# Two batches' own probabilities side by side: one 128x128 transpose in place of two in a fused Perceiver block

## The chip, the cores and the metric

The kernel runs on one core of one Trainium2 chip. The metric is device time of one execution in microseconds, lower is better. It is measured by repeated executions; one more execution was recorded by the profiler, and everything said of single instructions comes from that one.

## The reference, cut to what matters

The block has three parts in a row, each with a layer norm before it and a residual sum behind it: cross attention to a long context, causal self attention, and a mixture of eight experts of which two are used for each token. There are 8 batches of 64 tokens, width 256, 16 heads of 16.

```python
x = x + _L0_xattn_ref(_layernorm(x), ctx_1024, ctx_1024, ...)      # 1601 keys a batch
x = x + _L0_attn_ref(_layernorm(x), in_proj, out_proj)
x = x + _L0_ffn_ref(_layernorm(x), Wg, bg, W1, b1, W2, b2)         # 8 experts, top 2

# _L0_attn_ref, per batch and head, 64 x 64:
scores = jnp.einsum('bhqd,bhkd->bhqk', q / math.sqrt(D), k)
scores = jnp.where(causal[None, None], scores, -jnp.inf)
attn = jax.nn.softmax(scores, axis=-1)
out = jnp.einsum('bhqk,bhkd->bhqd', attn, v)
```

The change is in the self attention alone, between its softmax and its product with v.

## The kernel before, in words

**Tiles and steps.** Two batches make a tile of 128 token rows, so there are 4 tiles (0 to 3). The cross attention of a tile runs in 26 steps: for each of its two batches, 13 steps over blocks of up to 128 keys (k = 0 to 12; step s = 13 x batch + k). TensorE (PE) does in each step, in this order: the shift rows (L1382) and the scores (L1396) of the step, then "units" of other work, then `weigh` (L1216), the product of the last step's probabilities with the values. ScalarE (ACT) makes the exponentials (L739), GpSimd (POOL) adds them up in `prob_sum` (L490, four pieces a step). The exponential of a step waits for the sum of two steps before. In the last batch VectorE (DVE) does the sums. The denominators of a batch (`denominators`, L1415) are taken on PE in step k = 1 of the next batch, behind the last sum.

**Units.** A unit is a small piece of work that fills one PSUM bank and is read out by ACT or by DVE: "K" and "V" project keys and values of the batch to come, "M" finds score maxima (read by DVE at L923), "X" is the shift (L1256, behind DVE's `shift` at L865), "VL" are the last values. Between them stands the self attention and the router of the tile before, as a chain of units at steps written out by hand in `CHAIN_AT` (tiles 1 and 2), `CHAIN_AT_LAST` (tile 3) and `CHAIN_ALONE` (the tail behind tile 3, beside the first expert). So the chain of tile t runs within tile t + 1, and the program has it four times. The chain is: y1 (output projection), xt1, qk, v (projections), s0 and s1 (own scores of the two batches), the t units, o0 and o1 (product with v), y2, xt2, router, gt, b2.

**Banks.** Units take banks 2 to 6 in turn; a unit waits until the one that had its bank five units before has been read out. Tile 3 takes banks 4 to 6 in turn in its second half, the tail takes 6, 2, 7, 3. The first unit of a tile waits for all of the tile before.

**The softmax of the own scores.** DVE adds the mask to a batch's scores (L940), takes the row maxima (L841), subtracts them (L842); ACT takes the exponential in place (L670); two steps behind the scores DVE sums and divides the rows (L847 to L849) and raises `rows2_ready`. The result is `soft`, 128 rows by [2 batches, 8 head pairs, 64 keys]. A row is (one of two heads, query). The product with v needs keys on the rows, so the t units turn it.

**The t units.** Batch 0 is turned in t00 and t01 (step 12; step 11 in tile 3), batch 1 in t10 and t11 (step 14; step 13 in tile 3), all four at step 7 of the tail. A unit turns four 128x64 pieces into 64x128 and puts them on the upper (batch 0) or lower (batch 1) 64 rows of its bank. Batch 0's use the transpose operation (L1330, one pass of PE each). Batch 1's write rows 64 to 127 and are ordinary products with the identity (L1332), which for 32-bit data run as two passes each. ACT then copies 64 x 512 values a unit to `probs2` (L648), and o0 and o1 read that.

Of the kernel before, what the change touches and what calls it, by code (L numbers as in the profile page):

```python
# [12 lines left out]
P = 128  # L13
# [52 lines left out]
def in_order(counts):  # L66
    return {k: range(sum(n for j, n in counts.items() if j < k), sum(n for j, n in counts.items() if j <= k))
            for k in counts}
# [34 lines left out]
CHAIN_AT = {3: ["y1"], 5: ["xt1"], 6: ["qk", "v"], 8: ["s0"], 10: ["s1"], 12: ["t00", "t01"], 14: ["t10", "t11"],  # L103
            15: ["o0"], 16: ["o1"], 18: ["y2"], 20: ["xt2"], 21: ["router"], 24: ["gt"], 25: ["b2"]}

CHAIN_AT_LAST = {2: ["y1"], 4: ["xt1"], 5: ["qk", "v"], 7: ["s0"], 9: ["s1"], 11: ["t00", "t01"],
                 13: ["t10", "t11"], 15: ["o0", "o1"], 17: ["y2"], 19: ["xt2"], 20: ["router"], 23: ["gt"],
                 24: ["b2"]}
CHAIN_ALONE = {1: ["y1"], 2: ["xt1"], 3: ["qk"], 5: ["s0", "s1", "v"], 7: ["t00", "t01", "t10", "t11"],
               8: ["o0", "o1"], 9: ["y2"], 11: ["xt2"], 12: ["router"], 15: ["gt"], 16: ["b2"]}  # L110
ALONE_BANKS = [6, 2, 7, 3]
DONE_TILES = TT - 1
# [16 lines left out]
READ_BY_ACT = {"p1", "p2", "p3", "v", "V", "VL", "X", "xt1", "qk", "t00", "t01", "t10", "t11", "xt2", "router", "gt"}  # L129


class Units:
# [3 lines left out]
    def __init__(self, before, batch_after, chain, own=True, after_shift=len(V_AT[SHIFT_AT]), banks=RING_BANKS,  # L136
# [8 lines left out]
        for s in range(STEPS):  # L145
# [3 lines left out]
            for kind, u in row:  # L149
# [5 lines left out]
                     for n in range(len(order))]  # L155

# [125 lines left out]
def perceiver_kernel(nc, x, ctx_t, w_t, wg_t, biases, bo_row, bg_row, w1, b1, w2, b2, eye, masks, causal, out):  # L282
    stack = ExitStack()
    with stack:
# [48 lines left out]
        soft = sb("soft", [P, 2, G * PAIRS, Q])  # L333
# [265 lines left out]
        def _(act):  # L599
# [14 lines left out]
            def unit(units, n, kind, u, t, b, parity):  # L614
# [30 lines left out]
                elif kind[0] == "t":  # L645
                    bi, g = int(kind[1]), int(kind[2])
                    rows = slice(bi * Q, bi * Q + Q)
                    nc.scalar.activation(probs2[rows, g * 512:g * 512 + 512], src[rows, :], ACT.Copy)\  # L648
                        .then_inc(read_act, 1)
# [14 lines left out]
            def own_exponentials(units, s, t):  # L664

                for kind in units.chain.get(s - 1, []):
                    if kind in ("s0", "s1"):
                        bi = int(kind[1])
                        act.wait_ge(soft_ready, 2 * t + bi + 1)
                        nc.scalar.activation(soft[:, bi], soft[:, bi], ACT.Exp).then_inc(soft_exp_done, 1)  # L670
# [137 lines left out]
        def _(dve):  # L808
# [31 lines left out]
            def subtract_maxima(bi):  # L840
                link(nc.vector.tensor_reduce(neg_max2[:, bi], soft[:, bi], AX.X, ALU.max, negate=True))  # L841
                nc.vector.tensor_tensor(soft[:, bi], soft[:, bi], by_row(neg_max2[:, bi]), ALU.add).then_inc(soft_ready, 1)  # L842

            def divide_rows(bi, count):

                dve.wait_ge(soft_exp_done, count)
                link(nc.vector.tensor_reduce(row_sums2[:, bi], soft[:, bi], AX.X, ALU.add))  # L847
                link(nc.vector.reciprocal(row_sums2[:, bi], row_sums2[:, bi]))
                nc.vector.tensor_tensor(soft[:, bi], soft[:, bi], by_row(row_sums2[:, bi]), ALU.mult).then_inc(rows2_ready, 1)  # L849
# [765 lines left out]
```

## Time and profile before

| | us |
|---|---|
| median of 3 runs | 663.91 |
| lowest and highest | 663.18, 666.14 |
| the profiled execution | 663.55 |
| its span, first to last instruction | 661.7 |

Busy shares of the span: TensorE 95%, VectorE 72%, ScalarE 50%, GpSimd 46%. The span falls into a start (to 41 us), tile 0 (to 140), tile 1 (to 250), tile 2 (to 360), tile 3 (to 451), a tail with the fourth chain and the first expert (to about 494), and the seven other experts. PE is named apart as PE (products) and PEld (loading of the stationary operand, which overlaps). The distance between the starts of two products is what one costs when they stand in a row; the duration of a record is longer, as products are pipelined.

### The profile page before, as it was taken

The page shows a single profiled execution, that of the slowest core. Times are in us where ns is not written, and L with a number is a line of the kernel's source. Part 1 is how long each engine was busy: PE and PEld are TensorE (multiplying, and loading weights), DVE is VectorE, ACT ScalarE, POOL GpSimd, SP SyncE. Part 2 cuts the span into 40 slices and gives each one's busy share as a digit, 9 for nine tenths or more (in the row PEclk, how much of TensorE's full clock was granted, in tenths as well). Part 3 has the DMA queues.
Part 4 walks back from the last instruction along what each step waited for, and adds up shares of the span by engine and source line. Part 5 has one row for each costly group of instructions (what it writes and reads, how often), then busy time and mean ns, then how long its engine had stood idle before and what let it go on. Part 6 is the DMA issues. An engine that isn't in the chain of part 4 may idle for free.

```text
span 661.7 us, 15583 instructions
## 1 busy us (share of the span) xinstructions
PE 630.8 (95%) x6304; PEld 532.8 (81%) x6312; DVE 475.3 (72%) x878; ACT 329.4 (50%) x541; POOL 301.9 (46%) x386
## 2 busy tenths in 40 slices
PE   7989999999989989989998999978989999999997
PEld 4778878868877868877887888757879999999997
DVE  4887757667687678688777868686777666656753
ACT  4355655555554555446555545463654444444421
POOL 2138788897686688678678768200000000000000
PEclk9999999999989999999999999998989999999999
DMA  6311110100010010011110000423003302330000
GB/s 184 134 50 52 28 51 26 51 27 26 27 52 1 27 50 27 26 27 51 27 27 26 2 1 2 152 106 127 1 1 128 128 26 104 127 127 0 0 0 33
DMA packets 13285, 34.11 MB, mean 52 GB/s; under 512 B 1563, under 2 KB 10532, under 8 KB 11044
## 3 DMA queue, kind: packets, MB, share of 16 engines
q1 hardware_dynamic: 13188, 33.19, 15.1%
q8 instruction: 46, 0.75, 0.5%
q14 instruction: 19, 0.16, 0.1%
q0 software_dynamic: 32, 0.01, 0.0%
HBM read 32.67 MB, written 0.52 MB: 50 GB/s over the span
## 4 chain that ended last, share of the span: by engine, by line
PE 74%; DVE 13%; issue 5%; ACT 3%; POOL 3%; DMA 2%; SPq 0%; POOLq 0%; DVEq 0%; ACTq 0%
PE bank L1207 46%; PE bank L1396 8%; PE bank L1216 7%; PE bank L1382 4%; PE bank L1277 3%; POOL prob_sum L490 3%; DVE maxes L923 3%; DVE ctx_lo L474 2%; DMA raw<-in_w 1%; ACT k_hi L626 1%; DVE k_lo L904 1%; PE bank L1332 1%; PE bank L1320 1%; PE bank L1304 1%; DVE prob_sum L490 1%
## 5 line engine op out<-in xcount | busy, mean ns | idle before, releaser
L490 POOL TENSOR_TENSOR prob_sum<-probs,prob_sum 128x256 f32<-128x256 f32 x336 | 270.6, 837 | 71.4 <-ACT probs L739 66.4
L739 ACT ACTIVATE probs<-bank 128x1024 f32<-128x1024 f32 (+1 forms) x104 | 106.6, 1025 | 111.6 <-PE bank L1396 99.2
L923 DVE TENSOR_REDUCE maxes<-bank 128x1 f32<-128x400 f32 (+1 forms) x256 | 129.5, 564 | 20.3 <-PE bank L1277 19.8
L721 ACT ACTIVATE h_raw<-bank,b_sb 128x512 f32<-128x512 f32 (+2 forms) x72 | 46.2, 642 | 106.5 <-PE bank L1207 106.3
L904 DVE SCALAR_TENSOR_TENSOR k_lo<-bank,bias_sb,k_hi 128x400 fp32r<-128x400 f32 (+2 forms) x64 | 40.5, 632 | 48.6 <-ACT k_hi L626 48.6
L1207 PE MATMUL bank<-w_hi,h_hi 128*128 128x256 f32 x256 | 73.6, 288 | 0.8 <-DVE h_lo L1142 0.8
L1207 PE MATMUL bank<-w_lo,h_hi 128*128 128x256 f32 x256 | 72.9, 285 | 0.0
L1207 PE MATMUL bank<-w_hi,h_lo 128*128 128x256 f32 x256 | 72.8, 284 | 0.0
L1216 PE MATMUL bank<-probs,v_sb 128*32 128x128 f32 (+1 forms) x1664 | 68.1, 282 | 1.0 <-ACT probs L739 0.5
L1141 DVE CAST h_hi<-h_raw 128x512 fp32r<-128x512 f32 (+2 forms) x72 | 28.5, 396 | 55.5 <-ACT h_raw L721 54.1
L1207 PE MATMUL bank<-wv_hi,ctx_hi 128*128 128x256 f32 (+1 forms) x208 | 65.3, 314 | 2.6 <-DVE maxes L923 2.4
L1396 PE MATMUL bank<-qbd_hi,k_hi 64*128 64x256 f32 (+1 forms) x416 | 67.1, 318 | 0.0
L1277 PE MATMUL bank<-k_hi,qbd_hi 64*128 64x400 f32 (+1 forms) x256 | 58.5, 444 | 1.0 <-DVE qbd_hi L881 0.4
L1396 PE MATMUL bank<-qbd_lo,k_hi 64*128 64x256 f32 (+1 forms) x416 | 59.0, 279 | 0.0
L1396 PE MATMUL bank<-qbd_hi,k_lo 64*128 64x256 f32 (+1 forms) x416 | 58.9, 278 | 0.0
L1207 PE MATMUL bank<-wv_lo,ctx_hi 128*128 128x256 f32 (+1 forms) x208 | 58.7, 282 | 0.0
L1207 PE MATMUL bank<-wv_hi,ctx_lo 128*128 128x256 f32 (+1 forms) x208 | 58.4, 281 | 0.0
L629 ACT ACTIVATE v_sb<-bank 128x256 f32<-128x256 f32 (+1 forms) x104 | 39.7, 382 | 37.1 <-PE bank L1207 33.4
L626 ACT ACTIVATE k_hi<-bank,bias_sb 128x400 fp32r<-128x400 f32 (+2 forms) x64 | 38.1, 596 | 38.7 <-PE bank L1207 38.7
L1207 PE MATMUL bank<-xn_hi,w_hi 128*128 128x512 f32 (+2 forms) x144 | 55.0, 382 | 0.0
L1207 PE MATMUL bank<-xn_hi,w_lo 128*128 128x512 f32 (+2 forms) x144 | 54.8, 380 | 0.0
L1207 PE MATMUL bank<-xn_lo,w_hi 128*128 128x512 f32 (+2 forms) x144 | 54.6, 379 | 0.0
(155 smaller groups left out, 1389.8 us busy)
## 6 DMA issues: line engine op xcount, KB each, us to landing
raw<-in_w SPq DMA_DIRECT2D x16, 1024.0 KB, 6.8
ctx_raw<-in_ctx_t SPq DMA_DIRECT2D x16, 400.0 KB, 3.6
ctx_raw<-in_ctx_t SPq DMA_DIRECT2D x8, 402.0 KB, 3.8
ctx_raw<-in_ctx_t SPq DMA_DIRECT2D x8, 399.0 KB, 3.6
w_sb<-in_w_t SPq DMA_DIRECT2D x1, 1280.0 KB
w_raw<-in_w_t SPq DMA_DIRECT2D x2, 256.0 KB, 4.7
result<-x_all SPq DMA_DIRECT2D x4, 128.0 KB, 2.0
x_all<-in_x SPq DMA_DIRECT2D x1, 384.0 KB, 4.1
```

Of the source, the lines that this page charges most:

```text
L490: ins = engine.tensor_tensor(prob_sum[0:ROWS[k], cols], probs[0:ROWS[k], s % 2, cols], acc[0:ROWS[k]], ALU.add)
L626: nc.scalar.activation(k_hi[parity][:, g, EDGE[c]:EDGE[c + 1]], src[:, EDGE[c] - CH[c]:CW], ACT.Identity, bias=bias_sb[:, 1, g:g + 1]).the ...
L629: nc.scalar.activation(v_sb[0:ROWS[u], u * D:u * D + D], src[0:ROWS[u], 0:D], ACT.Copy).then_inc(read_act, 1)
L721: nc.scalar.activation(h_raw[:, c % 2, 0:width], bank[:, at, 0:width], ACT.Gelu, bias=b1_sb[:, bass.ds(e, 1), c:c + 1].rearrange("p a b -> ...
L739: nc.scalar.activation(probs[0:ROWS[k], s % 2, :].rearrange("p (g n) -> p g n", g=G), bank[0:ROWS[k], score_bank(b, k):score_bank(b, k) + ...
L904: nc.vector.scalar_tensor_tensor(out=k_lo[parity][:, g, EDGE[c]:EDGE[c + 1]], in0=src[:, EDGE[c] - CH[c]:CW], scalar=bias_sb[:, 1, g:g + 1 ...
L923: nc.vector.tensor_reduce(maxes[:, g * PAIRS + j, c:c + 1], src[:, 0:width], AX.X, ALU.max).then_inc(read_dve, 1)
L1141: link(nc.vector.tensor_copy(h_hi[:, c % 4, 0:width], h_raw[:, c % 2, 0:width]))
L1207: last = nc.tensor.matmul(dst, lhs, rhs, start=(start and n == 1), stop=(stop and n == 3 * len(pairs)), **more)
L1216: ins = nc.tensor.matmul(dst_bank[32 * j:32 * j + 32, (at + g) * P:(at + g + 1) * P], lhs(g, j), p_rows[:, m * P:(m + 1) * P], start=(star ...
L1277: ins = nc.tensor.matmul(dst[:, 0:width], qbd_hi[rows, parity, g, 2 * i:2 * i + 2, :].rearrange("p s q -> p (s q)"), k_hi[parity][rows, g, ...
L1396: ins = nc.tensor.matmul(bank[0:rows, score_bank(b, k) + r, g * RH * Q:(g + 1) * RH * Q], stays, moves, start=False, stop=(part == 2), ski ...
```

## The change

`soft` becomes [8 head pairs, 2 batches, 64 keys], so that the two batches' rows for a head pair lie side by side as 128 columns. One transpose of 128x128 turns both: the upper 64 rows of the result are batch 0's keys, the lower 64 batch 1's. The units t00, t01, t10, t11 become t0 and t1, which stand where t10 and t11 stood; at the steps of t00 and t01 nothing stands. Both wait for both batches' rows. The copies by ACT take 128 rows. DVE's and ACT's instructions on `soft` keep their number and size, but now step over the other batch's 64 columns. A tile has two units fewer, so the turn of the banks shifts; in the tail the banks of gt and b2 are set by a table.

```diff
-CHAIN_AT = {..., 10: ["s1"], 12: ["t00", "t01"], 14: ["t10", "t11"],
+CHAIN_AT = {..., 10: ["s1"], 14: ["t0", "t1"],
-CHAIN_AT_LAST = {..., 9: ["s1"], 11: ["t00", "t01"],
-                 13: ["t10", "t11"], 15: ["o0", "o1"], ...
+CHAIN_AT_LAST = {..., 9: ["s1"], 13: ["t0", "t1"],
+                 15: ["o0", "o1"], ...
-CHAIN_ALONE = {..., 5: ["s0", "s1", "v"], 7: ["t00", "t01", "t10", "t11"],
+CHAIN_ALONE = {..., 5: ["s0", "s1", "v"], 7: ["t0", "t1"],
+GATE_BANKS = {"gt": 3, "b2": 6}
...
+        if banks is ALONE_BANKS:
+            for n, kind in enumerate(order):
+                self.bank[n] = GATE_BANKS.get(kind, self.bank[n])
...
-        soft = sb("soft", [P, 2, G * PAIRS, Q])
+        soft = sb("soft", [P, G * PAIRS, 2, Q])
...
                 elif kind[0] == "t":
-                    bi, g = int(kind[1]), int(kind[2])
-                    rows = slice(bi * Q, bi * Q + Q)
-                    nc.scalar.activation(probs2[rows, g * 512:g * 512 + 512], src[rows, :], ACT.Copy)\
-                        .then_inc(read_act, 1)
+                    g = int(kind[1])
+                    nc.scalar.activation(probs2[:, g * 512:g * 512 + 512], src, ACT.Copy).then_inc(read_act, 1)
...
-                        nc.scalar.activation(soft[:, bi], soft[:, bi], ACT.Exp).then_inc(soft_exp_done, 1)
+                        nc.scalar.activation(soft[:, :, bi, :], soft[:, :, bi, :], ACT.Exp).then_inc(soft_exp_done, 1)
...
-                link(nc.vector.tensor_reduce(row_sums2[:, bi], soft[:, bi], AX.X, ALU.add))
+                link(nc.vector.tensor_reduce(row_sums2[:, bi], soft[:, :, bi, :], AX.X, ALU.add))
...
                 elif kind[0] == "t":
-                    bi, g = int(kind[1]), int(kind[2])
-                    pe.wait_ge(rows2_ready, 2 * t + bi + 1)
+                    g = int(kind[1])
+                    pe.wait_ge(rows2_ready, 2 * t + 2)
                     for j in range(PAIRS):
-                        turned, own_rows = dst[bi * Q:bi * Q + Q, j * P:j * P + P], soft[:, bi, g * PAIRS + j, :]
-                        if bi == 0:
-                            ins = nc.tensor.transpose(turned, own_rows, ident[:, :])
-                        else:
-                            ins = nc.tensor.matmul(turned, own_rows, ident[:, :], start=True, stop=True)
+                        ins = nc.tensor.transpose(dst[:, j * P:j * P + P],
+                                                  soft[:, g * PAIRS + j].rearrange("p b q -> p (b q)"), ident[:, :])
...
-                    units.wait_read_act(pe, read_act, f"t{bi}1")
+                    units.wait_read_act(pe, read_act, "t1")
```

Of DVE's instructions (L841, L842, L847, L849, L940) one stands for all; the others change in the same way.

On TensorE, step 12 of tile 1 stood so before: the scores of a short block of 65 keys, t00 and t01 (`ident,soft`), and the value unit.

```order
L1396 MATMUL bank<-qbd_hi,k_hi 65x256 x2
L1396 MATMUL bank<-qbd_lo,k_hi 65x256 x2
L1396 MATMUL bank<-qbd_hi,k_lo 65x256 x2
L1330 MATMUL bank<-ident,soft 64x128 x8
L1207 MATMUL bank<-wv_hi,ctx_hi 128x256
L1207 MATMUL bank<-wv_lo,ctx_hi 128x256
```

And so now, with line numbers of the changed file:

```order
L1394 MATMUL bank<-qbd_hi,k_hi 65x256 x2
L1394 MATMUL bank<-qbd_lo,k_hi 65x256 x2
L1394 MATMUL bank<-qbd_hi,k_lo 65x256 x2
L1208 MATMUL bank<-wv_hi,ctx_hi 128x256
L1208 MATMUL bank<-wv_lo,ctx_hi 128x256
```

The eight transposes are gone, and the value unit stands right behind the scores. On TensorE in step 14 of tile 1, t10 and t11 stood between the key unit (`ctx`, `wk`) and the unit of the last values:

```order
L1207 MATMUL bank<-ctx_hi,wk_hi 128x402
L1207 MATMUL bank<-ctx_lo,wk_hi 128x402
L1207 MATMUL bank<-ctx_hi,wk_lo 128x402
L1332 MATMUL bank<-ident,soft 64x128 x8
L1207 MATMUL bank<-wv_hi,ctx_hi 65x256
L1207 MATMUL bank<-wv_lo,ctx_hi 65x256
```

Now t0 and t1 stand in the same place:

```order
L1208 MATMUL bank<-ctx_hi,wk_hi 128x402
L1208 MATMUL bank<-ctx_lo,wk_hi 128x402
L1208 MATMUL bank<-ctx_hi,wk_lo 128x402
L1329 MATMUL bank<-ident,soft 128x128 x8
L1208 MATMUL bank<-wv_hi,ctx_hi 65x256
L1208 MATMUL bank<-wv_lo,ctx_hi 65x256
```

Nothing has moved there but the form: 128 rows of result in place of 64, by the transpose operation.

## Rows read from the trace of the kernel before

**Rows 1.** The page, part 1: busy us, share of span, instructions
```profile
PE 630.8 (95%) x6304; PEld 532.8 (81%) x6312; DVE 475.3 (72%) x878; ACT 329.4 (50%) x541; POOL 301.9 (46%) x386
```
**Rows 2.** Busy us of each engine in tiles 1 and 2 and most of 3
```profile
146.50:410.00 263.50, 254.50 (x3001) 212.98 (x3005) 204.10 (x352) 139.32 (x224) 198.61 (x251) 0.99 0.09 25
```
**Rows 3.** Chain that ended last, tile 1: start us, us, what
```profile
192.83 0.99 PE bank L1330 x8
...
202.24 1.96 PE bank L1332 x16
```
**Rows 4.** The two t lines: duration ns min/median/max, first and last start us
```profile
L1330 PE MATMUL bank<-ident,soft x32: 271/273/300, 192.8 to 473.5; 128*64 128x128 f32 x32
L1332 PE MATMUL bank<-ident,soft x64: 272/273/323, 202.2 to 476.0; 128*64 128x128 f32 x64
```
**Rows 5.** Timeline of PE, tile 1: start us, us [idle before <-releaser]
```profile
161.56 0.38 PE L1231 MATMUL bank<-ident,xn 128*128 128x128 f32 x2
...
192.76 1.06 PE L1330 MATMUL bank<-ident,soft 128*64 128x128 f32 x8
193.58 0.36 PE L1207 MATMUL bank<-wv_hi,ctx_hi 128*128 128x256 f32 x1
...
202.24 1.96 PE L1332 MATMUL bank<-ident,soft 128*64 128x128 f32 x16
204.13 0.34 PE L1207 MATMUL bank<-wv_hi,ctx_hi 128*65 128x256 f32 x1
```
**Rows 6.** Timeline of PE, tile 2, step 12
```profile
303.03 1.04 PE L1330 MATMUL bank<-ident,soft 128*64 128x128 f32 x8 [0.22 <-DVE soft L849]
303.82 0.36 PE L1207 MATMUL bank<-wv_hi,ctx_hi 128*128 128x256 f32 x1
```
**Rows 7.** Timeline, tile 1, steps 12 to 15, POOL, PE, DVE
```profile
194.35 4.25 POOL L490 TENSOR_TENSOR prob_sum<-probs,prob_sum 65x256 f32<-65x256 f32 x4 [0.17 <-ACT probs L739]
...
199.86 0.65 PE L1216 MATMUL bank<-prob_sum,ones_f 128*32 128x128 f32 x16
...
201.61 2.02 DVE L923 TENSOR_REDUCE maxes<-bank 128x1 f32<-128x402 f32 x4
...
206.18 2.03 DVE L923 TENSOR_REDUCE maxes<-bank 128x1 f32<-128x402 f32 x4 [0.76 <-PE bank L1277]
```
**Rows 8.** Timeline, tile 3, steps 10 to 14, POOL, DVE, PE
```profile
406.77 10.37 POOL L490 TENSOR_TENSOR prob_sum<-probs,prob_sum 128x256 f32<-128x256 f32 x12 [0.21 <-ACT probs L739]
...
408.18 1.54 DVE L865 TENSOR_TENSOR shift<-ident,neg_max 128x1024 bf16<-128x1024 f32 x1
...
410.67 0.38 PE L1256 MATMUL bank<-shift,ones_bf 128*128 128x512 bf16 x1 [0.16 <-issue]
...
418.92 0.65 PE L1216 MATMUL bank<-prob_sum,ones_f 128*32 128x128 f32 x16
```
**Rows 9.** Timeline of the tail, step 7, DVE and PE
```profile
473.47 0.69 DVE L849 TENSOR_TENSOR soft<-soft,row_sums 128x512 f32<-128x512 f32 x1
...
474.30 1.93 PE L1332 MATMUL bank<-ident,soft 128*64 128x128 f32 x16 [0.52 <-DVE soft L849]
```
**Rows 10.** Two ACT copies out of PSUM, columns as in group 4
```profile
L648 ACT ACTIVATE probs<-bank x16: 577/592/597, 194.2 to 476.3; 64x512 f32<-64x512 f32 x16
L633 ACT ACTIVATE shift_rows<-bank x16: 576/597/626, 38.7 to 411.4; 128x512 bf16<-128x512 f32 x16
```
**Rows 11.** Two DVE lines, columns as in group 4
```profile
L904 DVE SCALAR_TENSOR_TENSOR k_lo<-bank,bias_sb,k_hi x64: 618/634/639, 11.1 to 394.6; 128x400 fp32r<-128x400 f32 x32, 128x402 fp32r<-128x402 f32 x16, 128x399 fp32r<-128x399 f32 x16
L855 DVE SCALAR_TENSOR_TENSOR masked<-bank,mask_sb,masked x8: 483/484/485, 96.0 to 452.3; 128x256 f32<-128x256 f32 x8
```
**Rows 12.** Two stretches: PE, PEld, DVE, ACT, POOL busy, clock, DMA share, GB/s
```profile
185.80:189.10 3.30, 3.30 (x30) 2.57 (x30) 3.23 (x4) 0.39 (x1) 3.11 (x4) 0.50 0.46 124
192.80:196.20 3.40, 3.40 (x47) 2.91 (x46) 3.40 (x4) 2.71 (x7) 3.23 (x4) 1.00 0.02 5
```
**Rows 13.** Timeline of PE ahead of the first of these stretches
```profile
183.95 2.00 PE L1320 MATMUL bank<-k_t,qbd 128*128 128x64 f32 x16 [1.77 <-issue]
```

More of the change, by code:

```diff
@@ L101 @@
 LAST_V_AT = 1
-CHAIN_AT = {3: ["y1"], 5: ["xt1"], 6: ["qk", "v"], 8: ["s0"], 10: ["s1"], 12: ["t00", "t01"], 14: ["t10", "t11"],
+CHAIN_AT = {3: ["y1"], 5: ["xt1"], 6: ["qk", "v"], 8: ["s0"], 10: ["s1"], 14: ["t0", "t1"],
             15: ["o0"], 16: ["o1"], 18: ["y2"], 20: ["xt2"], 21: ["router"], 24: ["gt"], 25: ["b2"]}
[L106 to L109, printed above, removed]
+CHAIN_AT_LAST = {2: ["y1"], 4: ["xt1"], 5: ["qk", "v"], 7: ["s0"], 9: ["s1"], 13: ["t0", "t1"],
+                 15: ["o0", "o1"], 17: ["y2"], 19: ["xt2"], 20: ["router"], 23: ["gt"], 24: ["b2"]}
+CHAIN_ALONE = {1: ["y1"], 2: ["xt1"], 3: ["qk"], 5: ["s0", "s1", "v"], 7: ["t0", "t1"],
                8: ["o0", "o1"], 9: ["y2"], 11: ["xt2"], 12: ["router"], 15: ["gt"], 16: ["b2"]}
 ALONE_BANKS = [6, 2, 7, 3]
+GATE_BANKS = {"gt": 3, "b2": 6}
 DONE_TILES = TT - 1
@@ L126, in both_tiles @@
     return [("M", ROW_TILES * u + r) for u in pairs for r in range(ROW_TILES)]
-READ_BY_ACT = {"p1", "p2", "p3", "v", "V", "VL", "X", "xt1", "qk", "t00", "t01", "t10", "t11", "xt2", "router", "gt"}
+READ_BY_ACT = {"p1", "p2", "p3", "v", "V", "VL", "X", "xt1", "qk", "t0", "t1", "xt2", "router", "gt"}
 class Units:
@@ L840, in subtract_maxima @@
             def subtract_maxima(bi):
-                link(nc.vector.tensor_reduce(neg_max2[:, bi], soft[:, bi], AX.X, ALU.max, negate=True))
-                nc.vector.tensor_tensor(soft[:, bi], soft[:, bi], by_row(neg_max2[:, bi]), ALU.add).then_inc(soft_ready, 1)
+                link(nc.vector.tensor_reduce(neg_max2[:, bi], soft[:, :, bi, :], AX.X, ALU.max, negate=True))
+                nc.vector.tensor_tensor(soft[:, :, bi, :], soft[:, :, bi, :], by_row(neg_max2[:, bi]), ALU.add).then_inc(soft_ready, 1)
             def divide_rows(bi, count):
                 dve.wait_ge(soft_exp_done, count)
-                link(nc.vector.tensor_reduce(row_sums2[:, bi], soft[:, bi], AX.X, ALU.add))
+                link(nc.vector.tensor_reduce(row_sums2[:, bi], soft[:, :, bi, :], AX.X, ALU.add))
                 link(nc.vector.reciprocal(row_sums2[:, bi], row_sums2[:, bi]))
-                nc.vector.tensor_tensor(soft[:, bi], soft[:, bi], by_row(row_sums2[:, bi]), ALU.mult).then_inc(rows2_ready, 1)
+                nc.vector.tensor_tensor(soft[:, :, bi, :], soft[:, :, bi, :], by_row(row_sums2[:, bi]), ALU.mult).then_inc(rows2_ready, 1)
             def own_heads(src, read, count):
@@ L938, in unit @@
                 elif kind in ("s0", "s1"):
-                    nc.vector.tensor_tensor(soft[:, int(kind[1])], src.rearrange("p (n k) -> p n k", k=Q),
+                    nc.vector.tensor_tensor(soft[:, :, int(kind[1]), :], src.rearrange("p (n k) -> p n k", k=Q),
                                             causal_sb[:, :].unsqueeze(1).broadcast_to([P, G * PAIRS, Q]),
```

## The prediction

> **What bounds the kernel now.** I read the page's busy shares first: PE is busy 95% of the span, DVE 72%, ACT 50%, POOL 46% [rows 1]. The shares of the stretch in which three of the four chains run say more: from 146.5 to 410 us PE is busy 254.5 of 263.5 us, DVE 204.1, POOL 198.6 and ACT 139.3 [rows 2]. So PE is the bound there, but two others are at about three quarters, and each can be the one waited for at single steps. Next I asked whether the instructions that the change touches are on the path. The chain that ended last runs through both of tile 1's groups, 0.99 us at L1330 and 1.96 us at L1332 [rows 3]. The reader is to see that no wait stands between them and their neighbours in tile 1: behind L1330 the value unit starts at once, at 193.58 [rows 5]. Work taken out of such a row is time taken out, until something else is late.
>
> **The price of one transpose.** A record lasts 273 ns at both lines [rows 4], but they overlap. L1330's eight span 1.06 us, so their distance is (1.06 - 0.27) / 7 = 0.11 us; L1332's sixteen give (1.96 - 0.27) / 15 = 0.11 us [rows 5]. One pass is thus 0.11 us, and batch 1's products take two passes each. The new form is 128x128. The trace has it at L1231, where two in a row span 0.38 us with the same 273 ns each, again 0.11 us apart [rows 5, 4]. Bounds for the new one: 0.109, as L1231 has it, and 0.27, if eight in a row did not overlap at all. I take 0.11, since L1231 is the same operation with the same operand sizes; two in a row are thin evidence for eight, but L1332's sixteen keep the same distance. A tile has 8 + 16 = 24 passes before and 8 after: 16 x 0.11 = 1.76 us less of PE a tile, 7.0 us for four chains. That is the ceiling; now what each place lets through.
>
> The Trainium skill, page "TensorE: Matmul & The Clock Gate", section "Part 4: PE-mode transpose", gives about 275 ns for a transpose of 128x128 in one kernel's context. The trace agrees as to the duration and not as to the distance. Were that figure the cost of each, a tile would save 16 x 0.275 = 4.4 us and the kernel would end some 11 us below my forecast.
>
> **Tiles 1 and 2.** Step 12 loses t00 and t01: from 192.76 to 193.58, 0.82 us [rows 5]. In tile 2 the same unit starts at 303.03 after 0.22 us of waiting for DVE's division of batch 0, and the next one at 303.82 [rows 6]. The wait goes too: 0.79 + 0.22 = 1.01 us. Step 14 keeps eight passes of sixteen, 8 x 0.11 = 0.87 us less in each. Sum 0.82 + 1.01 + 2 x 0.87 = 3.57 us.
>
> What is late next? First POOL. Its sum of step 12 ends at 194.35 + 4.25 = 198.60, and PE takes the denominators at 199.86 [rows 7]. Their place moves up by 0.82 to 199.04, so 0.44 us of the slack remains. Then DVE. In step 14 it reduces the four maxima in 2.02 us from 201.61; that is behind the denominators and moves with them [rows 7]. In step 15 its next maxima start at 206.18 after 0.76 us idle. That start may move by 0.87 more than DVE's earlier work does; 0.76 of it is idle time, so at most 0.11 us is lost there, and DVE idles again soon after. I count nothing for it. The new wait, on both batches' rows instead of one's, stands where batch 1's stood already, so nothing is queued behind a later event than before. I went through the bank of each unit: from step 14 on each follows the same kind as before, and the five that follow the two removed units get banks that have been free for longer.
>
> **Tile 3.** Step 11 loses 0.8 us, but PE then comes to X, which waits for DVE's shift: that ends at 408.18 + 1.54 = 409.72, and X started at 410.67, with about 0.25 us between release and start [rows 8]. X can move to about 409.98, so 0.69 us come through. Step 13 gives 0.87. POOL adds up steps 10, 11 and 12 in one run of 10.37 us, to 417.14, and the denominators stand at 418.92 [rows 8]: 1.56 us earlier is 417.36, just behind the sum. Sum 1.56 us, with 0.2 us of cover left; the range must allow for its failing.
>
> **Tail.** Here batch 0's eight passes ran while DVE was still dividing batch 1's rows (473.47 to 474.16), and batch 1's started at 474.30 after a wait of 0.52 us for that [rows 9]. Taking batch 0's away only lengthens the wait. Batch 1's sixteen become eight behind the same event: 0.87 us, not 1.76.
>
> **ACT and DVE.** ACT makes two copies of 128 rows for four of 64. Rows cost it nothing: 64x512 takes 592 ns and 128x512 takes 597 [rows 10]. It gets 1.2 us a tile back, which PE and POOL hide, as nobody waits for it in steps 12 and 14; if that cover were gone it would be a further gain. DVE's and ACT's instructions on `soft` now step over 64 columns after every 64. Is that dearer? L855 reads a PSUM bank in just such pieces: 484 ns for 256 columns. L904 reads without gaps: 634 ns for 400. Both have the same kind of scalar operand. The difference, 150 ns for 144 columns, is 1.04 ns a column, which leaves 484 - 266 = 218 ns and 634 - 416 = 218 ns of fixed cost [rows 11]. So gaps cost nothing that can be seen. Nothing that reads and writes SBUF in such pieces stands in the trace, so zero is taken by the nearest row, and the other end is a rival below.
>
> **The sum.** 3.57 + 1.56 + 0.87 = 6.0 us. The profiled execution took 663.55, so it would take 657.55. The median of the runs is 0.36 us above it: **657.9 us**, 0.9% less.
>
> **Rivals.**
> 1. *The gain in step 12 does not come through.* If POOL or DVE is late at the places above, because DVE's operations and POOL's stretch when they fall together in a new way, the 0.82, 1.01 and 0.69 us are lost and 3 x 0.87 + 0.87 = 3.5 us remain: 660.4 us. For it speaks the thin cover, 0.44 and 0.2 us. Against it: POOL began both of those runs after waiting for an exponential, 0.17 and 0.21 us [rows 7, 8], so it was not behind when they started, and in tile 1 it has idle time again behind 198.60, until the denominators are taken.
> 2. *The gaps in `soft` cost DVE and ACT time, and the kernel is slower.* There are 10 DVE operations of 512 columns and 2 of ACT a tile. In the tail nearly all of them follow one another ahead of t0, and in tile 2 PE waits for them at step 12 [rows 6, 9]; I reckon 30 on the path in all. The change loses from 6.0 / 30 = 0.2 us an operation on. If a gap halved the rate, each would take 0.53 us more: 30 x 0.53 = 16 us, less 6.0, gives about 674 us. Rows 11 speak against it.
> 3. *More half-speed stretches.* The granted clock was 0.50 from 185.8 to 189.1 us, behind 1.77 us of idle PE [rows 12, 13], and there are more such stretches later in the run. Each can cost up to half of its 3.4 us, 1.7 us. Two more would give 657.9 + 3.4 = 661.3; one fewer 656.2. In the stretch behind tile 1's eight transposes the clock stayed at 1.00 [rows 12], so the transposes do not bring one on here. The same section of the Trainium skill says that the full clock does not engage for transposes; by that the eight new ones, in place of sixteen plain products, would invite one more such stretch a tile, and the trace does not bear it out.
> 4. *Passes are dearer in the new form.* At 0.27 us each the eight take 2.2 us, 1.3 more than I take, four times: 663 us, no change.
> 5. *All of the ceiling comes through*, with a little from ACT: 663.9 - 7.2 = 656.7 us; with one half-speed stretch fewer 655.0.
>
> **How the numbers follow.** Forecast, with its own spread from 656.0 to 659.8 (rival 5 without the clock lies in it): 0.60. Rival 1: 0.13. Rival 2, at any size that undoes the gain or worse: 0.06. Rival 3 upward: 0.08, downward 0.05. Rival 4: 0.03. A gain larger than the ceiling for a reason that I don't see: 0.05. The range takes in rivals 1, 3 and 5: **655.0 to 662.0**. Faster or slower by 0.5%, 3.3 us, is about what a measurement of this kernel can tell from no change; the lines are at 660.6 and 667.2. Below the first lie the forecast, rival 3 downward, the larger gain and half of rival 1: 0.76. Within: half of rival 1, most of 3 upward, 4, and the mild half of 2: 0.19. Above: 0.05.
>
> **What would show it.** In the profile after, eight records a tile at the t line (L1329), 32 in all, 0.11 us apart, eight in 1.04 us; rival 4 would show as 2.2 us. ACT's copies: 8 of about 597 ns. DVE's lines on `soft`: means as before, 0.68 to 0.69 us where POOL is quiet; rival 2 would show there at once. The value unit of step 12 right behind the scores, and the denominators of tile 3 not waiting for POOL; rival 1 shows as an idle PE ahead of them with POOL as the releaser. The distance between the same step of tile 1 and tile 2 shorter by about 1.7 us. What would make me wrong: a wait in a place that I did not look at, above all between steps 15 and 25, where I take all work to move up as one.

## The result and the profile after

The changed kernel takes 658.37 us (median of 4 runs, 656.94 to 659.16) against 663.92 before: a ratio of 0.9929, 95% interval 0.9900 to 0.9959. Two later measurements of the same kernel, each with more executions of the kernel before beside it, gave 658.67 against 662.81 (ratio 0.9936, 0.9913 to 0.9960) and 658.14 against 662.75 (0.9938, 0.9911 to 0.9965). Some executions take 6 to 13 us longer at a lower granted clock, whatever the kernel, and one of an experiment below took 2016 us; medians, means and ratios here are without them. So the change is faster by 0.6 to 0.7% by the ratios and by 4.1 to 5.5 us by the medians, where the forecast was 6.0 us. The time was forecast at 657.9, and the range 655.0 to 662.0 holds all three.

The page of the changed kernel's profiled execution: its span, part 1 (busy us, share of the span, instructions) and the engines' shares of part 4, the chain that ended last:

```profile
span 655.1 us, 15447 instructions
PE 626.0 (96%) x6248; PEld 526.5 (80%) x6248; DVE 474.7 (72%) x878; ACT 324.2 (49%) x533; POOL 301.2 (46%) x386
PE 73%; DVE 13%; issue 6%; POOL 3%; ACT 3%; DMA 2%; POOLq 0%; DVEq 0%; SPq 0%; ACTq 0%
```

Against [rows 1] PE has lost 4.8 us of busy time and ACT 5.2; DVE's 878 instructions take as long as before. The new t line and ACT's copies of its result in the changed kernel (duration ns min/median/max, first and last start us) answer to [rows 4, 10]:

```profile
L1329 PE MATMUL bank<-ident,soft x32: 272/273/331, 201.3 to 470.9; 128*128 128x128 f32 x32
L650 ACT ACTIVATE probs<-bank x8: 591/597/603, 202.0 to 471.2; 128x512 f32<-128x512 f32 x8
```

The timeline of PE in tile 1 of the changed kernel (start us, us) answers to [rows 5]; the first two lines are step 12, the last two step 14:

```profile
192.30 0.28 PE L1394 MATMUL bank<-qbd_hi,k_lo 64*65 64x256 f32 x2
192.51 0.38 PE L1208 MATMUL bank<-wv_hi,ctx_hi 128*128 128x256 f32 x1
...
201.28 1.14 PE L1329 MATMUL bank<-ident,soft 128*128 128x128 f32 x8
202.24 0.33 PE L1208 MATMUL bank<-wv_hi,ctx_hi 128*65 128x256 f32 x1
```

The value unit of step 12 stands right behind the scores. In step 14 the t units hold PE for 202.24 - 201.28 = 0.96 us, where it was 204.13 - 202.24 = 1.89 [rows 5].

Where the time went is read best from the starts of the exponentials, as each ends one step of PE. Here are those of steps 12 to 15 of tile 1, from ACT's timeline (start us, us, and at the end the idle time ahead and what ended it), before (L739) and after (L740):

```profile
193.25 1.03 ACT L739 ACTIVATE probs<-bank 65x1024 f32<-65x1024 f32 x1
196.18 1.03 ACT L739 ACTIVATE probs<-bank 128x1024 f32<-128x1024 f32 x1 [0.69 <-PE bank L1396]
199.97 1.02 ACT L739 ACTIVATE probs<-bank 128x1024 f32<-128x1024 f32 x1 [1.40 <-PE bank L1396]
206.89 1.02 ACT L739 ACTIVATE probs<-bank 128x1024 f32<-128x1024 f32 x1 [1.41 <-PE bank L1396]
```
```profile
192.98 1.02 ACT L740 ACTIVATE probs<-bank 65x1024 f32<-65x1024 f32 x1
195.21 1.03 ACT L740 ACTIVATE probs<-bank 128x1024 f32<-128x1024 f32 x1 [0.93 <-PE bank L1394]
199.01 1.02 ACT L740 ACTIVATE probs<-bank 128x1024 f32<-128x1024 f32 x1 [1.41 <-PE bank L1394]
205.00 1.02 ACT L740 ACTIVATE probs<-bank 128x1024 f32<-128x1024 f32 x1 [1.42 <-PE bank L1394]
```

The lead is 0.97 us at steps 13 and 14 and 1.89 at step 15, so step 14 gave 0.92. The lead was 0.26 to 0.27 at step 12, so the t units' leaving it gave 0.71. Done in the same way everywhere, for the first profile and for the one of the run `again` (for the tail, the starts of the first layer's activations ahead of it and behind it, in `again` alone, where both kernels have the same number of half-speed stretches between them):

| place | forecast us | first profile | second profile |
|---|---|---|---|
| tile 1, step 12 | 0.82 | 0.71 | 0.71 |
| tile 1, step 14 | 0.87 | 0.92 | 0.91 |
| tile 2, step 12 | 1.01 | 0.94 | 0.94 |
| tile 2, step 14 | 0.87 | 0.91 | 0.93 |
| tile 3, step 11 | 0.69 | 0.58 | 0.58 |
| tile 3, step 13 | 0.87 | 1.07 | 1.07 |
| tail | 0.87 | | 0.94 |
| sum | 6.00 | | 6.08 |

What else differs is the clock. Both profiles have a half-speed stretch in tile 2 that the profile before lacks; it costs 1.51 and 1.57 us of the 6. Two stretches of the changed kernel, one in tile 1 and this one in tile 2 (from and to us, length, busy us of PE, PEld, DVE, ACT and POOL, the granted clock, DMA share, GB/s):

```profile
185.80:189.10 3.30, 3.30 (x34) 2.57 (x34) 3.23 (x4) 0.38 (x1) 2.85 (x3) 0.50 0.45 124
295.10:298.40 3.30, 3.30 (x30) 2.66 (x29) 3.23 (x4) 0.38 (x1) 3.30 (x4) 0.50 0.45 124
```

At 0.50 the engine runs at 1.2 GHz, the lower of its two levels. The stretch in tile 1 is in both kernels [rows 12]. At the end of tile 3 the changed kernel has a longer one, some 10 us in one piece, in all three of its profiles; the profile before has two of 3.4 us there with full clock between them. The changed kernel, and the middle of that place in the kernel before, columns as above:

```profile
441.90:452.00 10.10, 8.65 (x71) 6.75 (x68) 7.30 (x14) 4.27 (x7) 0.00 (x0) 0.50 0.53 207
```
```profile
448.70:451.90 3.20, 1.47 (x33) 1.00 (x34) 1.93 (x3) 1.95 (x3) 0.00 (x0) 1.00 0.26 41
```

In the first profile a stretch in the tail, which the kernel before has at 486.1 us, is missing in turn; so its span is 6.6 us shorter, 655.1 for 661.7, where the medians differ by 5.5.

The timed executions say the same as these profiles. The mean granted clock of an execution is 0.987 over 18 of the changed kernel and 0.990 over the 55 of the kernel before that ran beside it and beside the experiments; 19 of the 55 reach 0.991 or more, and none of the 18 does. That is some 3 us more at half speed in each execution, worth 1.1 to 1.5 us by my estimate (0.45 us for each 0.001 of clock among the 55, and 1.5 us for a stretch of 3.4 us). It accounts for most of the way from the 6.1 us of the table to the 4.1 and 4.6 us of the two larger comparisons.

### The profile page after: what moved, and what is told of

Its sections match the earlier page's. It is cut to its first block, busy times and chain, and to the rows that moved or that the text cites. A ratio compares the mean times of both kernels' runs of the same rounds, so it can differ in the third digit from the quotient of the medians.

```text
span 655.1 us, 15447 instructions
## 1 busy us (share of the span) xinstructions
PE 626.0 (96%) x6248; PEld 526.5 (80%) x6248; DVE 474.7 (72%) x878; ACT 324.2 (49%) x533; POOL 301.2 (46%) x386
## 4 chain that ended last, share of the span: by engine, by line
PE 73%; DVE 13%; issue 6%; POOL 3%; ACT 3%; DMA 2%; POOLq 0%; DVEq 0%; SPq 0%; ACTq 0%
PE bank L1208 45%; PE bank L1394 8%; PE bank L1217 7%; PE bank L1380 4%; DVE maxes L924 3%; PE bank L1278 3%; POOL prob_sum L493 3%; DVE ctx_lo L477 1%; DMA raw<-in_w 1%; PE bank L1321 1%; DVE prob_sum L493 1%; ACT k_hi L629 1%; DVE k_lo L905 1%; DVE shift L866 1%; PE bank L1305 1%
## 5 line engine op out<-in xcount | busy, mean ns | idle before, releaser
L740 ACT ACTIVATE probs<-bank 128x1024 f32<-128x1024 f32 (+1 forms) x104 | 106.6, 1025 | 111.8 <-PE bank L1394 99.4
```

What stands on the lines that cost most here:

```text
L740: nc.scalar.activation(probs[0:ROWS[k], s % 2, :].rearrange("p (g n) -> p g n", g=G), bank[0:ROWS[k], score_bank(b, k):score_bank(b, k) + ...
```

## Experiments: is it the passes, and which of them?

**The layout alone.** The kernel before, with the new shape of `soft` and nothing else:

```diff
-        soft = sb("soft", [P, 2, G * PAIRS, Q])
+        soft = sb("soft", [P, G * PAIRS, 2, Q])
...
-                        turned, own_rows = dst[bi * Q:bi * Q + Q, j * P:j * P + P], soft[:, bi, g * PAIRS + j, :]
+                        turned, own_rows = dst[bi * Q:bi * Q + Q, j * P:j * P + P], soft[:, g * PAIRS + j, bi, :]
```

> The kernel before with the new layout of soft alone: [8 head pairs, 2 batches, 64 keys], all four t units at their old steps, with their old operations. Theory (gaps cost nothing): as before, 663.9 us within 1 us, and the means of the ten DVE operations and two ACT operations a tile as before (about 0.68 us where GpSimd is quiet, 0.63 us on ACT). Rival (gaps cost time): at 0.2 us an operation with some 30 on the path, 670 us; the means of those lines show it directly.

Measured: 661.71 us, against 662.81 for the kernel before beside it, ratio 0.9989 (0.9965 to 1.0012). DVE's and ACT's instructions on `soft` in that kernel, by tile (duration ns min/median/max):

```profile
L940 DVE TENSOR_TENSOR soft<-bank,causal_sb x8: 673/680/692, 178.4 to 467.8; 128x512 f32<-128x512 f32 x8
L842 DVE TENSOR_TENSOR soft<-soft,neg_max x8: 691/952/1206, 179.8 to 469.2; 128x512 f32<-128x512 f32 x8
L670 ACT ACTIVATE soft<-soft x8: 622/626/632, 181.2 to 469.9; 128x512 f32<-128x512 f32 x8
L849 DVE TENSOR_TENSOR soft<-soft,row_sums x8: 691/959/1239, 190.6 to 472.3; 128x512 f32<-128x512 f32 x8
```

And the same instructions in the kernel before, without gaps:

```profile
L940 DVE TENSOR_TENSOR soft<-bank,causal_sb x8: 675/680/692, 178.1 to 468.9; 128x512 f32<-128x512 f32 x8
L842 DVE TENSOR_TENSOR soft<-soft,neg_max x8: 692/959/1216, 179.5 to 470.3; 128x512 f32<-128x512 f32 x8
L670 ACT ACTIVATE soft<-soft x8: 622/626/632, 180.9 to 471.1; 128x512 f32<-128x512 f32 x8
L849 DVE TENSOR_TENSOR soft<-soft,row_sums x8: 691/955/1222, 190.3 to 473.5; 128x512 f32<-128x512 f32 x8
```

Line by line the medians are within 1% of each other; those of the maxima (L841) are 686 ns in both. Steps over 64 columns cost nothing here, on either engine; rival 2 is gone.

**The operation.** The changed kernel with the plain product for the transpose, of the same size and in the same place:

```diff
-                        ins = nc.tensor.transpose(dst[:, j * P:j * P + P],
-                                                  soft[:, g * PAIRS + j].rearrange("p b q -> p (b q)"), ident[:, :])
+                        ins = nc.tensor.matmul(dst[:, j * P:j * P + P],
+                                               soft[:, g * PAIRS + j].rearrange("p b q -> p (b q)"), ident[:, :],
+                                               start=True, stop=True)
```

> The changed kernel with the transpose operation replaced by the plain product with the identity, of the same 128x128: two passes for one. Theory (passes count, 0.11 us each): 8 x 0.11 = 0.87 us more in each of four chains, 658.4 + 3.5 = 661.9 us. Rival (what gave the gain is the lower number of instructions or of units, not passes): 658.4. Rival on the clock (transposes bring half-speed stretches on, products do not): fewer such stretches than with transposes.

**Each transpose twice.**

```diff
+                        for _ in range(2):
                             ins = nc.tensor.transpose(...)
```

> The changed kernel with each of the eight transposes issued twice to the same place. Theory: 8 x 0.11 = 0.87 us more a chain, 661.9 us, as the run with products; step 14 to 15 longer by 0.87 us in each tile. Rival (repeats are hidden by another engine): 658.4. Rival on the clock: more half-speed stretches than in the run with products, as there are 16 transposes a tile.

Measured: 661.27 us with products (ratio 0.9997, 0.9959 to 1.0034) and 660.60 with doubled transposes (0.9982, 0.9955 to 1.0008), against 658.67 for the changed kernel beside them (`again`). PE's timeline in step 14 of tile 1 (start us, us), first the kernel with products, then the one with doubled transposes:

```profile
201.66 2.05 PE L1329 MATMUL bank<-ident,soft 128*128 128x128 f32 x16
```
```profile
200.04 1.97 PE L1330 MATMUL bank<-ident,soft 128*128 128x128 f32 x16
201.77 0.36 PE L1208 MATMUL bank<-wv_hi,ctx_hi 128*65 128x256 f32 x1
```

Both have sixteen passes a tile. By the starts of the exponentials both keep the gain of step 12 (0.70 and 0.73 us in tile 1, 0.94 and 0.95 in tile 2) and lose that of step 14 (0.07 and 0.16 in place of 0.92). So the gain of step 14 is the number of passes: the doubled transposes need 201.77 - 200.04 = 1.73 us for sixteen, 0.11 us each in a row of sixteen. In tiles 1 and 2 the loss is 0.85 and 0.76 us each, near the 0.87; in tile 3 it is 0.98 and 0.88, and the tail gains 0.1 and 0.2 us over the kernel before where the changed kernel gains 0.94. That is some 3.5 and 3.2 us for the four chains, as expected.

The median times, 2.6 and 1.9 us above the changed kernel, fall short of that. In the mean the kernel with products is 3.7 us above (661.95 of 10 executions, 658.28 of all 18 of the changed kernel), the one with doubled transposes 2.1; but of the latter's ten executions four had a granted clock of 0.994, which none of the 18 reached. So the half-speed stretches, which differ between executions, hide part of the loss. The times alone would not have settled the question.

**Batch 0's units left out, in the tiles and in the tail.** In the kernel before:

```diff
-CHAIN_AT = {..., 10: ["s1"], 12: ["t00", "t01"], 14: ["t10", "t11"],
+CHAIN_AT = {..., 10: ["s1"], 14: ["t10", "t11"],
```

> The kernel before without t00 and t01 in the chains of tiles 1 to 3 (the turning of batch 0 is left out there, and o0 reads batch 1's rows instead); the tail as before. Theory: 0.82 + 1.01 + 0.69 = 2.5 us less, 661.4 us. Rival (that place is covered by GpSimd or VectorE): no change, 663.9.

```diff
-CHAIN_ALONE = {..., 7: ["t00", "t01", "t10", "t11"],
+CHAIN_ALONE = {..., 7: ["t10", "t11"],
```

> The kernel before without t00 and t01 in the tail alone (left out there: the turning of batch 0; o0 reads what the chain before left). Theory: they run while VectorE still divides batch 1's rows, so nothing is saved: 663.9 us, and the wait ahead of t10 grows from 0.5 to about 1.6 us. Rival: 0.87 us less, 663.0; by the timed runs alone these two can't be told apart, by the profile's timeline they can.

(This kernel also has the changed kernel's table of banks for gt and b2 in the tail, and o0 waits there for t11's copy.)

Without them in the tiles: 662.38 us, against 662.42 beside it, ratio 1.0006 (0.9959 to 1.0053). By the time it is no change. By the starts of the exponentials it is 0.72, 0.95 and 0.60 us less, 2.3 in all, just the share of step 12 in the changed kernel; a stretch of half speed that is 6.8 us long in tile 2 takes 3 us back in the profiled execution. The time was inconclusive, the profile was not. Without them in the tail: 663.17 us, ratio 1.0011 (0.9988 to 1.0035), and PE's timeline there shows the wait that the theory named (start us, us, in brackets the idle time ahead and its releaser):

```profile
473.06 1.93 PE L1336 MATMUL bank<-ident,soft 128*64 128x128 f32 x16 [1.60 <-DVE soft L853]
```

It was 0.52 us with them in place [rows 9]. Eight passes ahead of that event are free there. PE's timeline of the changed kernel has the same wait, and half of the work behind it:

```profile
470.08 1.06 PE L1329 MATMUL bank<-ident,soft 128*128 128x128 f32 x8 [1.61 <-DVE soft L850]
```

**How much further would it go?** The changed kernel with one of four transposes:

```diff
-                    for j in range(PAIRS):
+                    for j in range(1):
```

> The changed kernel with one of four transposes in each t unit; the turning of the other three head pairs is left out. Theory: 6 x 0.11 = 0.66 us less in each chain, 658.4 - 2.6 = 655.8 us. Rival: the cover that GpSimd had in tile 3 (0.2 us by the sum) is used up, and step 14 there waits for the sum of step 12: then 0.5 us of that does not come through, and the releaser of the denominators there is GpSimd.

Measured: 657.21 us in the median of four, ratio 0.9899 (0.9852 to 0.9947). Of 6 x 0.11 = 0.66 us a chain, 2.6 us in all, the median is 1.2 below the 658.4 of all 18 executions of the changed kernel; by the profile it is some 0.5, of which 0.35 lie in the tail. In step 14 the gain over the kernel before is 0.93 us in tiles 1 and 2, the same as with eight passes. The reason is in that kernel's timeline of PE, tile 1:

```profile
201.40 0.33 PE L1329 MATMUL bank<-ident,soft 128*128 128x128 f32 x1
201.88 0.33 PE L1329 MATMUL bank<-ident,soft 128*128 128x128 f32 x1 [0.15 <-DVE maxes L924]
202.36 0.33 PE L1208 MATMUL bank<-wv_hi,ctx_hi 128*65 128x256 f32 x1 [0.15 <-DVE maxes L924]
```

t0, t1 and the value unit need banks that DVE frees one by one, and they start 201.88 - 201.40 = 202.36 - 201.88 = 0.48 us apart whatever they hold. Four transposes take 0.44 us. So the changed kernel sits just at that floor, and fewer passes bring nothing in step 14. And in tile 3, where the gain was 1.19 us for 1.07, the same kernel's PE waits for the sum of POOL, as the rival had it:

```profile
415.04 0.64 PE L1217 MATMUL bank<-prob_sum,ones_f 128*32 128x128 f32 x16 [0.49 <-POOL prob_sum L493]
```

## Experiments: the idle time ahead of s1

The kernel before idles 1.77 us on PE ahead of s1 in tile 1 [rows 13], and a half-speed stretch stands behind it. PE's timeline of the changed kernel shows the same in tile 2, ahead of the stretch at 295.1:

```profile
293.56 2.30 PE L1321 MATMUL bank<-k_t,qbd 128*128 128x64 f32 x16 [1.77 <-issue]
```

Since t0 and t1 are not due before step 14, s1 can stand a step later:

```diff
-CHAIN_AT = {3: ["y1"], 5: ["xt1"], 6: ["qk", "v"], 8: ["s0"], 10: ["s1"], 14: ["t0", "t1"],
+CHAIN_AT = {3: ["y1"], 5: ["xt1"], 6: ["qk", "v"], 8: ["s0"], 11: ["s1"], 14: ["t0", "t1"],
```

> The changed kernel with the scores of the second batch (s1) one step later, at 11 in place of 10, in tiles 1 and 2; this has room because t0 waits at step 14 for both batches. In both profiles PE idles 1.77 us ahead of s1 for VectorE's spreading of the queries, and a half-speed stretch follows in tile 1. Theory: both idle times go, 658.4 - 3.5 = 654.9 us, and with one or two half-speed stretches fewer (1.5 us each) 652 to 653.5. Rival: VectorE is what is late there, and the wait comes back ahead of X or of t0: 658.

Measured: 654.47 us, ratio 0.9868 (0.9828 to 0.9909). That is near the 654.9 that I had for the idle times alone, and above the 652 to 653.5 with the stretches gone too. The wait ahead of s1 is gone, and so is the stretch: here PE's timeline of tile 1 (start us, us), and then busy times and clock of the stretch around it, with the columns as above. The granted clock is 1.00, which is 2.4 GHz:

```profile
184.86 0.28 PE L1394 MATMUL bank<-qbd_hi,k_lo 64*128 64x256 f32 x2
185.07 2.00 PE L1321 MATMUL bank<-k_t,qbd 128*128 128x64 f32 x16
```
```profile
184.00:190.00 6.00, 5.84 (x73) 4.78 (x69) 5.86 (x9) 3.14 (x5) 5.75 (x5) 1.00 0.23 68
```

Then four kernels side by side on one chip: the kernel before with the same move, the changed kernel with it once more, that with one more edit in the tail, and the changed kernel as it is.

> The kernel before (sixteen transposes and products in four units) with s1 one step later in tiles 1 and 2. Theory: the idle time ahead of s1 goes here too, and with it the half-speed stretches in tiles 1 and 2; against the changed kernel with the same move (654.5 us) it is slower by what the change gives by itself where no half-speed stretch differs: 1.6 + 1.9 + 1.6 + 0.9 = 6.0 us, so 660.5 us. Rival (the change gives less once the idle time is gone, or the move needs the change): the two are within 3 us.

> The changed kernel with s1 at step 11, once more beside the others. Theory: 654.5 us, and again no half-speed stretch in tiles 1 and 2. Rival (the absence of such stretches in its first profile was luck): one is there, and the time is 1.5 us more for each.

> As that, and in the tail PE does the first layer's chunk 6 of the first expert ahead of t0 instead of behind t1. PE idles 1.6 us there for VectorE's division; the chunk takes 1.05 us. Theory: 1.0 us less, 653.5 us. Rival: the chain of the tail is held later by something that does not move (xn, 0.8 us idle), and nothing is gained.

> The changed kernel beside these. 658.4 us; a half-speed stretch in tile 1 or 2 behind the idle time ahead of s1.

| kernel | median us | ratio to before (95%) |
|---|---|---|
| before, s1 at 11 | 658.72 | 0.9931 (0.9905 to 0.9957) |
| changed, s1 at 11 | 654.50 | 0.9870 (0.9777 to 0.9964) |
| the same, tail swapped | 655.20 | 0.9842 (0.9767 to 0.9917) |
| changed | 658.14 | 0.9938 (0.9911 to 0.9965) |

**The move alone.** It works without the change as well, by 0.7%, as much as the change itself. In none of the profiles of the three kernels with s1 at step 11, four in all, is there a half-speed stretch in tiles 1 and 2. Of the ten profiles with s1 at step 10, before and changed and the experiments above, eight have at least one. So the stretches of tiles 1 and 2 go with the idle time ahead of s1, whichever form the t units have. It is not certain to bring one on, since two of the ten profiles have none; and that it is the cause, and not something else that the move shifts, is not shown. The timed executions agree less clearly: the mean clock of the kernel before rises from 0.990 to 0.992 with the move, yet four of its nine executions are still at 0.989, so those still have more of the half speed somewhere.

The exponential of step 15 in tile 1 shows how the gain divides. In `before_s1` it starts 2.63 us earlier than in the kernel before (the start of the profile taken off). A half-speed stretch there is worth 1.5 us (the changed kernel's first profile and its third, which has none, part by that much at step 11), so 1.1 us of the 1.77 of idle time are gained for good. In the changed kernel less is gained: against its third profile, without a stretch, `s1_again` leads by 3.53 - 3.18 = 0.35 us only, and by 0.38 us more in tile 2, where I had expected 1.77 us in each. What PE waits for instead in that kernel, in steps 12 and 13 of tile 1:

```profile
195.36 0.39 PE L1380 MATMUL bank<-shift_rows,ones_bf 64*128 64x512 bf16 x2 [0.64 <-ACT probs L740]
...
197.42 0.64 PE L1217 MATMUL bank<-prob_sum,ones_f 128*32 128x128 f32 x16 [0.37 <-POOL prob_sum L493]
```

So of the 3.6 us by which the move betters the changed kernel 0.7 are the wait that it takes away, and most of the rest goes with the clock: both profiles of the changed kernel with the move have one stretch of 3.4 us at the end of tile 3 too, where the changed kernel has 10 us.

**The change on top of the move** gives 658.72 - 654.50 = 4.2 us, where I expected 6.0. By the medians that is no less than without the move (4.1 to 5.5 us), but it is made up in another way: without the move 6.1 us came off the steps and the clock took some back; here 4.5 us came off the steps. What fell away is step 12: with s1 a step later the removal there brings nothing, since the wait of 0.64 us for the exponential, above, has taken its place. The kernel before with the move has the eight passes there and no such wait, only the one for POOL (its timeline of PE, same place):

```profile
195.80 0.39 PE L1382 MATMUL bank<-shift_rows,ones_bf 64*128 64x512 bf16 x2
...
197.76 0.64 PE L1216 MATMUL bank<-prob_sum,ones_f 128*32 128x128 f32 x16 [0.38 <-POOL prob_sum L490]
```

What is left, by the exponentials, is step 14 (0.90 and 0.92 us), tile 3 (1.65) and the tail (1.06), 4.5 us.

**The tail swapped.** The edit puts one chunk of the first layer ahead of t0, to fill the 1.6 us of waiting:

```diff
             for s in range(LAST_ROWS_AT):
-                alone(s)
+                if s != 7:
+                    alone(s)
                 for c in FIRST_HIDDEN.get(s, []):
...
                     hidden(0, c, c % 2, 0, DONE_TILES)
+                if s == 7:
+                    alone(s)
```

It gave nothing that can be seen: the median is 655.20 against 654.50, the ratio is better, 0.9842 against 0.9870, and with four executions each (one of `s1_again` took 661.73 us) neither difference is clear of noise. Its timeline of PE around t0 and t1:

```profile
466.00 1.06 PE L1329 MATMUL bank<-ident,soft 128*128 128x128 f32 x8 [0.54 <-DVE soft L850]
467.89 0.17 PE L1337 MATMUL bank<-ident_bf,ones_bf 128*128 128x8 bf16 x1 [0.83 <-ACT probs L650]
```

The wait ahead of t0 shrank by 1.06 us, as meant. But the chunk had covered ACT's two copies between t1 and o0, and now PE waits 0.83 us for those. One more half-speed stretch at 468.7 us, which its profile has, cost 1.5 us there. No kernel of the study is shown to be faster than the changed one with s1 at step 11.

## The remaining expectation

> The changed kernel once more, for a second profile. 658 us. The starts of the exponentials, step by step, should move against the kernel before by 0.7 and 0.9 us in tile 1, 0.9 and 0.9 in tile 2, 0.6 and 0.9 in tile 3, as in its first profile; what differs between the two profiles should be only the half-speed stretches. Rival: the new half-speed stretch in tile 2 (295 us) belongs to the change; then it is there again.

The shares of the steps agree within 0.02 us between the two profiles. The stretch at 295 us was there again; but in the third profile of the changed kernel (`after_third`) neither it nor the one in tile 1 is there, and the kernel with the layout alone, which has the transposes of before, has one at 296.7 us. So it comes and goes with the execution. That the changed kernel has more of such stretches on average is shown above; what in the change brings them is open. The kernels with products, with doubled transposes and without batch 0's units in the tiles, which all leave step 12 without t units, have a mean clock of 0.986, 0.988 and 0.986; the kernels with the layout alone and with the tail alone changed have 0.991 and 0.989.

## Why the prediction was right, point by point

- **The bound.** PE was the one to shorten: outside the tail nearly every pass taken away came off the steps. Of the ceiling of 7.0 us 6.1 came through there, and the free half in the tail is the 0.87 that did not. In the timed runs 4.1 to 5.5 us are left, for the clock took some back.
- **Luck in the number.** The 657.9 is only 0.5 us below the first median because it stands on 663.91, a median of three; the larger samples of the kernel before have 662.4 to 662.8, and 6.0 us less than 662.8 is 656.8, where the changed kernel took 658.1 to 658.7.
- **The price of a transpose**, 0.11 us from two in a row: right for rows of four (after) and of sixteen (doubled). The 273 ns of a record is not its cost. Had the 275 ns of the Trainium skill's page "TensorE: Matmul & The Clock Gate", section "Part 4: PE-mode transpose", been the price of each, the doubled kernel would have lost 2.2 us a chain; it lost 0.8 to 0.9. The page gives it as a duration, and for bf16.
- **Step 12** was put 0.1 us too high in each tile (0.82 for 0.71, 1.01 for 0.94, 0.69 for 0.58). In tile 1 the value unit did start 0.81 us earlier, 192.51 for 193.58, less the lead of 0.26. The rest was lost behind it. The shift rows and scores of step 13 start at 194.06, 0.65 us behind the start of `weigh`, where it was 0.58 in the kernel before (195.05 - 194.47). The exponential of step 12 ends just ahead of them, at 192.98 + 1.02 = 194.00:

```profile
193.41 0.64 PE L1217 MATMUL bank<-probs,v_sb 128*32 128x128 f32 x16
194.06 0.39 PE L1380 MATMUL bank<-shift_rows,ones_bf 64*128 64x512 bf16 x2
```

  So PE comes some 0.07 us too early for the end of that exponential. It is the place where a wait of 0.64 us for it stands with s1 at step 11. I had looked at POOL and DVE there and not at ACT.
- **Tile 3, step 11**: 0.58 us came through for 0.69, and that near only because two errors cancel. The product that I took for X's start (410.67, [rows 8]) is its second; the first has no record, but its weights were loaded at 410.44. So X could move by 0.46 us to my 409.98, and not by 0.69. But X starts 0.15 us behind the end of DVE's shift (405.95 + 1.54 = 407.49), not 0.25. The weight loads of the kernel before, and X in the changed kernel:

```profile
410.44 0.11 PEld L1256 LDWEIGHTS bank<-shift,ones_bf 128*128 128x128 bf16 x2 [0.20 <-ACT v_sb L629]
```
```profile
407.64 0.59 PE L1257 MATMUL bank<-shift,ones_bf 128*128 128x512 bf16 x2 [0.27 <-DVE shift L866]
```

- **Tile 3, step 13** was put 0.2 us too low (0.87 for 1.07). I had the distance of passes only. In the kernel before, the value unit behind t11 also waited there for one of ACT's copies, as its weight loads show:

```profile
416.40 0.19 PEld L1207 LDWEIGHTS bank<-wv_hi,ctx_hi 128*128 128x128 f32 x1 [0.17 <-ACT probs L648]
```

  The removal of that copy, which I had counted at nothing, gave the 0.2.
- **The cover in tile 3** was real and used up to the last: the sum of POOL ends at 404.53 + 10.39 = 414.92, and PE takes the denominators at 415.04. My 0.2 us was 0.1. POOL's and PE's timelines of the changed kernel:

```profile
404.53 10.39 POOL L493 TENSOR_TENSOR prob_sum<-probs,prob_sum 128x256 f32<-128x256 f32 x12 [0.24 <-ACT probs L740]
...
415.04 0.65 PE L1217 MATMUL bank<-prob_sum,ones_f 128*32 128x128 f32 x16
```

- **Steps 15 to 25 of tile 3**, where I took all work to move up as one, do hold a wait. In step 22 `weigh` waits for the exponential of step 21, ahead of which ACT does a piece of the experts' weights (L714 in the changed kernel):

```profile
433.93 0.64 PE L1217 MATMUL bank<-probs,v_sb 128*32 128x128 f32 x16 [0.16 <-ACT probs L740]
```
```profile
438.20 0.65 PE L1216 MATMUL bank<-probs,v_sb 128*32 128x128 f32 x16 [0.55 <-ACT probs L739]
```

  The first is the changed kernel, the second the kernel before. The wait is in six of the seven profiles of kernels with eight passes or fewer (0.16 to 0.40 us), and of the seven others only in that of the kernel before. So the comparison with that one profile hides it, and the change may lose up to 0.4 us there; with so few profiles that is not shown.
- **The tail**: batch 0's passes were free, batch 1's half was not. The kernel `no_b0_tail` shows the first, and the second shows in the 0.94 us of the table, most of which the kernels with products and doubled transposes lose again.
- **The half-speed stretches** (rival 3) did happen, one more in tile 2, at 1.5 us where I had put a ceiling of 1.7, and a longer one at the end of tile 3. In the first profile one less in the tail made up for it, by luck: over all executions the changed kernel has some 3 us more at half speed. The transpose operation did not bring them on, as far as these runs show: the kernel with plain products had one of 6.8 us in tile 2, the one with sixteen transposes none at all in tiles 1 and 2. Busy times and clock of the products' kernel in that stretch, and of the doubled transposes' from 180 to 300 us:

```profile
295.40:302.00 6.60, 6.60 (x48) 5.68 (x47) 6.06 (x9) 0.38 (x1) 4.30 (x4) 0.50 0.22 62
```
```profile
180.00:300.00 120.00, 114.21 (x1377) 94.34 (x1377) 96.08 (x162) 63.68 (x103) 93.79 (x118) 1.00 0.12 32
```

  The same section of the Trainium skill says that the full clock does not engage for transposes; the granted clock, at 1.00 throughout the doubled row, does not bear that out for rows of sixteen between other products. No transpose of this size stands in a half-speed stretch, so what the full clock is worth to one is not shown.
- **Rivals 1, 2 and 4** did not occur, apart from the 0.1 us of step 12, which ACT took and not POOL or DVE. Rival 1 was close in tile 3, with 0.12 us between POOL's end and the denominators, and DVE's banks held the floor of 0.48 us a unit in tiles 1 and 2.

## What to carry to other kernels

Price a short PE operation by the distance between starts in a row, not by its duration, and count passes: a plain product of 32-bit data is two. For each place ask separately what is late next; here seven places gave between 0.58 and 1.07 us for eight passes each, and in tiles 1 and 2 there was nothing more to give, as `quarter` shows. When single half-speed stretches move the time by 1.5 us, compare two profiles step by step at a regular event, here the exponentials: that told 0.1 us apart where timed runs could not tell 2 us. Two profiles are still two executions: look at the granted clock of all of them before a difference of stretches is put down to chance.

## What I had not expected of the hardware

A stretch of half speed hardly moves when work is taken out: in the profiles with s1 at step 10 it lies at 185.6 to 186.1 us in tile 1 and at 294.8 to 296.7 in tile 2, or is missing, and lasts 3.4 us or twice that. One of 3.4 us cost 1.5 us. PE had been idle for 1.77 us some 2 us ahead of it. With that idle time gone, four profiles of four have none there; that it is the cause is likely and not shown. And a unit that is not waited for, moved by one step, was worth as much as taking away two thirds of the transposes' passes.
